# Weighted values of two attention steps in one block, with three buffers of probabilities

## The reference

```
h = layernorm(x) * (1 + ca) + sa                      # x: 4 x 1024 x 256
qkv = h @ w_qkv.T + b_qkv                             # 16 heads of 16
attn = softmax(q @ k.T / sqrt(16))                    # 4 x 16 x 1024 x 1024
x = x + ga * ((attn @ v) @ w_o.T + b_o)
... # a second layer norm, routing of each token to 6 of 32 experts, shared expert
```

## Time and profile before

| | us |
|---|---|
| median of 3 runs | 1539.56 |
| lowest and highest | 1530.76, 1542.15 |
| span of the profiled execution (first to last instruction) | 1412.3 |
| median less span | 127.3 |
| TensorE busy | 1342.8 (95%) |
| VectorE busy | 1134.9 (80%) |
| ScalarE busy | 753.7 (53%) |

### The profile page before, as it was taken

The page is one execution under the profiler, slowest core; times in us unless marked ns, Lnnn a source line. Parts: engine busy times, 40 slices in busy tenths (PEclk is TensorE's granted clock), DMA queues, the critical chain, the costliest instruction groups (busy, mean ns, idle before and its releaser), DMA issues.

```text
span 1412.3 us, 30839 instructions
## 1 busy us (share of the span) xinstructions
PE 1342.8 (95%) x8191; PEld 672.8 (48%) x8192; DVE 1134.9 (80%) x2823; ACT 753.7 (53%) x1155; POOL 606.9 (43%) x782
## 2 busy tenths in 40 slices
PE   7997999999999999999999999999999999999895
PEld 4552222332333323323333232568788888888551
DVE  7886999999999999999999994566566656656588
ACT  3762477676767676777677768113343433334100
POOL 4000113143644534636346357527755555655300
PEclk9997799999999999999999999999999999999999
DMA  6898355533546345444464355947766665666698
GB/s 218 260 270 216 93 171 133 121 85 83 125 126 156 91 121 149 132 96 107 125 170 117 105 155 176 274 136 234 231 199 206 202 183 177 180 179 178 238 344 337
DMA packets 216958, 243.55 MB, mean 172 GB/s; under 512 B 93948, under 2 KB 181500, under 8 KB 216736
## 3 DMA queue, kind: packets, MB, share of 16 engines
q1 hardware_dynamic: 189328, 166.42, 43.6%
q0 software_dynamic: 21776, 68.07, 13.4%
q10 hardware_dynamic: 5760, 7.87, 1.7%
HBM read 133.98 MB, written 108.28 MB: 172 GB/s over the span
## 4 chain that ended last, share of the span: by engine, by line
PE 71%; DVE 13%; DMA 4%; issue 1%; SPq 1%; ACT 1%; POOL 0%; DVEq 0%; POOLq 0%
PE psO L1174 14%; PE ex_psGU L1682 13%; PE psE L1161 13%; PE psM L1151 9%; DVE piece_max L1048 9%; PE ex_psY L1697 7%; PE ex_psX L1671 3%; PE psM L505 2%; PE ex_psA L1691 2%; PE psGU L1495 1%; DMA wide<-results 1%; PE co_psS L1951 1%; PE late_psGU L1931 1%; PE late_psX L1942 1%; PE psM L524 1%
## 5 line engine op out<-in xcount | busy, mean ns | idle before, releaser
L1048 DVE TENSOR_REDUCE piece_max<-psM 128x1 f32<-128x512 f32 x1024 | 641.9, 680 | 27.3 <-PE psM L1151 24.0
L1115 ACT ACTIVATE wide<-psE 128x1024 f32<-128x1024 f32 x512 | 496.8, 1021 | 206.2 <-PE psE L1161 204.1
L1151 PE MATMUL psM<-wide 48*128 48x512 bf16 x1024 | 324.0, 395 | 19.9 <-DVE piece_max L1048 11.7
L1161 PE MATMUL psE<-wide 49*128 49x512 bf16 (+1 forms) x2048 | 328.7, 380 | 3.2 <-DMA wide<-maxima 2.8
L1763 POOL DMA_INDIRECT results<-vals_inv,places x223 | 213.9, 959 | 150.5 <-DVE vals_inv L1749 86.4
L1174 PE MATMUL psO<-wide 128*32 128x512 f32 x2048 | 273.6, 606 | 0.6 <-ACT wide L1115 0.6
L1151 PEld LDWEIGHTS psM<-wide 48*128 48x128 bf16 x1024 | 78.1, 93 | 348.1 <-DVE piece_max L1048 277.3
L1682 PE MATMUL ex_psGU<-wide,ex_xT 128*128 x892 | 231.3, 382 | 0.8 <-ACT ex_xT L1714 0.7
L1161 PEld LDWEIGHTS psE<-wide 49*128 49x128 bf16 (+1 forms) x2048 | 117.6, 95 | 92.3 <-issue 8.7
L1682 PEld LDWEIGHTS ex_psGU<-wide,ex_xT 128*128 128x128 f32 x892 | 152.1, 190 | 14.6 <-issue 2.3
L1714 ACT ACTIVATE ex_xT<-ex_psX 128x256 f32<-128x256 f32 x223 | 85.3, 383 | 121.3 <-PE ex_psX L1671 118.5
(11 more groups left out here) (281 smaller groups left out, 1262.8 us busy)
## 6 DMA issues: line engine op xcount, KB each, us to landing
wide<-qk_parts SPq DMA_DIRECT2D x384, 64.0 KB
wide<-results SPq DMA_DIRECT2D x16, 1536.0 KB, 9.5
rows<-lists SPq DMA_DIRECT2D x112, 160.0 KB
h2Ts<-lists SPq DMA_DIRECT2D x111, 160.0 KB
qk_parts<-parts SPq DMA_DIRECT2D x32, 384.0 KB, 3.1
xin<-in_x_dram SPq DMA_DIRECT2D x16, 512.0 KB, 4.2
v_values<-vst SPq DMA_DIRECT2D x32, 256.0 KB, 3.5
wide<-v_values SPq DMA_DIRECT2D x16, 512.0 KB
```

The costliest lines, as they stand in the source:

```text
L1048: v.tensor_reduce(piece_max[:, qh, (x * PAIRS + h) * KT // QH + qt, kh:kh + 1], bank_of("piece", PIECES * group + n), AX.X, ALU.max, negat ...
L1115: nc.scalar.activation(probs[:, step % 2, 2 * pair:2 * pair + 2], psE[:, pair], ACT.Exp, scale=HD ** -0.5).then_inc(exp_ok, 1)
L1151: nc.tensor.matmul(bank_of(*user), qa[g][rows, h, qt * P:(qt + 1) * P], ka[g][rows, h, kh * 512:(kh + 1) * 512], start=True, stop=True).th ...
L1161: mm = nc.tensor.matmul(psE[:, pair, x], k[g][part, pair, kt * P:(kt + 1) * P], q[g][part, pair, qh * 512:(qh + 1) * 512], start=(q is qa) ...
```

## The change

`probs` becomes a list of three buffers instead of two. The third stands in `h2Ts`. `weighted_values` is no longer called once in each step for the step before, but twice in a row in each even step, for the two steps before; after the loop it is called for the last two. Exp waits for `summed` to reach step - 2 instead of step - 1. Since `h2Ts` is now in use until the end of attention, the contents of the spare rows move to a part of `x2`, GpSimd waits for `spare_in` before its loop over chunks, and SyncE loads `h2Ts` only once `summed` has reached 255.

```diff
-        probs = env.wide[:, GPART * NG:].rearrange("p (n h q) -> p n h q", n=2, h=HG)
+        probs = [*(env.wide[:, GPART * NG + HG * 512 * n:GPART * NG + HG * 512 * (n + 1)].rearrange("p (h q) -> p h q", h=HG)
+                   for n in range(2)), env.h2Ts[:].rearrange("p n k t -> p (n k) t")]
...
-        spare_to = env.h2Ts[:, 0].rearrange("p k t -> p (k t)").bitcast(I32).rearrange("p (e f) -> p e f", e=E)
+        spare_to = env.x2[:, TPC * (LAST - 1):TPC * LAST].rearrange("p i d -> p (i d)").bitcast(I32).rearrange(
+            "p (e f) -> p e f", e=E)
...
-            sp.wait_ge(spare_in, 16 * (E + 1))
+            sp.wait_ge(summed, ALL - 1)
             for n in range(2):
                 sp.wait_ge(env.h2T_out, 16 * (n + 1))
                 sp.dma_start(env.h2Ts[:, n], env.h2T_d[n]).then_inc(env.h2T_in[n], 16)
...
             add_bias(0)
+            pool.wait_ge(spare_in, 16 * (E + 1))
             for c in range(LAST):
...
                     if pair == 0:
-                        wait(act, summed, step - 1)
-                    nc.scalar.activation(probs[:, step % 2, 2 * pair:2 * pair + 2], psE[:, pair], ACT.Exp,
+                        wait(act, summed, step - 2)
+                    nc.scalar.activation(probs[step % 3][:, 2 * pair:2 * pair + 2], psE[:, pair], ACT.Exp,
                                          scale=HD ** -0.5).then_inc(exp_ok, 1)
...
-                                          probs[:, s % 2, 2 * pair + x], start=(kt == 0), stop=(kt == KT - 1))
+                                          probs[step % 3][:, 2 * pair + x], start=(kt == 0), stop=(kt == KT - 1))
...
-                if step:
+                if step and step % 2 == 0:
+                    weighted_values(step - 2)
                     weighted_values(step - 1)
                 if to < NGR:
                     piece(to, first + 2)
                     piece(to, first + 3)
                 route_products(step)
+            weighted_values(ALL - 2)
             weighted_values(ALL - 1)
```

## The result

| | us |
|---|---|
| before, median of 4 runs | 1540.74 (1530.76 to 1542.15) |
| after, median of 4 runs | 1631.07 (1628.08 to 1636.37) |
| ratio, 95% interval | 1.0605 [1.0548, 1.0662] |
| profiled execution after | 1630.02, span 1628.3, mean granted clock 0.956 |

The change costs 90.3 us. The prediction said 1629.6.

The account below looks back on a forecast made before the run. The prediction took a loop through TensorE and VectorE, 2.49 us a step, to bound attention. Terms 79.5 + 7 + 2.5 + 1 = +90 us gave a span of 1502, with 127.3 around it 1629.6 us; range 1612 to 1650.

Parts of the forecast that it names:

- the step from P1 to P2: In plain even steps, TensorE's piece 2 starts 2.22 us behind piece 1, with two sets of weighted values between.
- the loop of a pair: Two plain attention steps, through TensorE and VectorE: 5.80 us against 4.97 before, a price of +0.82 us a pair.
- the lower bound named for this term: Price of a plain pair if the second set's passes come 0.43 us apart: +0.78 us.
- blocks beside other work of VectorE's: Where VectorE selects experts, steps 26 to 29 of a window, its work fills the gap: about 0.1 us a block.
- exp's wait, the spare rows and the loads: Looser exp wait and GpSimd's new wait: zero each; later loads of `h2Ts` behind attention: +1 us, bounds 0 and +4.
- the loops together: Attention's longer pairs: 79.5 us for 97 plain pairs, 7 for other blocks, 2.5 for the last 11 steps.
- the mixed steps: Steps 12 and 30 of a window, gap partly filled: 0.4 and 0.5 us; with the expert-selection blocks +7 us in all.
- the clock: Rival: TensorE's granted clock drops for a tenth of the time in attention, +35 us, 1665 us; chance 0.03.
- 60% of filled places at a clock of 1.00: Evidence against a clock drop: from 405 to 417 us TensorE's places fill some 60% of the step at full clock.
- with 127.3 around the span: Time taken to lie outside the profiled span, 127.3 us, added to the predicted span of 1502 us.
- the first rival: In attention, with VectorE work banked for the block, saved array switches make it faster: -23 us, 1516 us; chance 0.03.

Follow-up runs that it names:

- the occasion at 1417 us: The runs of the first seven experiments, where the unedited kernel before takes 1417 to 1419 us; the result and the last five experiments have it at 1540 to 1545.
- the stand-in: The changed kernel with blocks of two only in steps 26 and 28 of windows 1 to 6, single sets elsewhere: 1541.26 us against 1541.95 for the kernel before.

## Why the prediction was right, and where not

**Right: the step from P1 to P2 and the loop of a pair.** P2 is 2.17 us behind P1 (2.22 predicted), its reduction 0.42 behind it, the rest of the loop as written: 5.74 us for 5.80. The passes of the second set are 0.43 apart and those of the first 0.45, so the lower bound named for this term holds, +0.78. Taking the block away brings the old time back, 24 plain blocks cost 17.0 us where 24 times the price is 18.5, and one bank less costs one reduction a step. The mechanism is shown.

**Right: blocks beside other work of VectorE's.** Twelve of them changed the time by -0.7 us, where +0.1 each was predicted; neither can be told from nothing. **Right: exp's wait, the spare rows and the loads**: 0.5 us with everything in place but the blocks, and 0.6 us more on the chain behind attention with them; +1 was predicted, and neither can be told from nothing.

**Mis-sized: the loops together.** 79.5 + 7 + 2.5 = 89 predicted, some 82 or 83 measured, by the 0.04 to 0.05 us a pair of the second set's passes, 97 times, and a rest of some 2 or 3 us in the mixed steps.

**Wrong: the clock**, given 0.03, +35 us, with "the clock should stay at 1.00". It falls to half in 12 to 14 stretches of attention and costs about 29 us on the occasion at 1417 us, where it was counted; on that of the result, where a kernel with hardly a block has six such stretches itself, the change adds some 10 us by it (an estimate). The step that failed is the evidence taken from the earlier trace rows: 60% of filled places at a clock of 1.00. The block changes how idle time lies, not only how much of it there is: places that were spread now lie closer, with longer pauses between. That this is what brings the fall is my reading and is not shown: 6 of 14 such pauses bring none, and three falls have none ahead. What is shown is that a fall that meets a block doubles 1.86 us and starves VectorE for 2.56. As a rival it had about the right size for the occasion at 1417 us and too small a chance. The same paragraph has the active share of a plain pair fall from 87% to 75%, which was reason for a wider range upward.

**Wrong: "with 127.3 around the span".** Some 2 us lie around a span. The profile and the timed runs were of two occasions, and the 127.3 us were a longer time inside the span of the timed runs: the stand-in's span there is 1535.7 us, with 751.0 in attention and 452.9 in the expert loop for 726.3 and 372.1. On the occasion of the profile the sum should have read 90 - 7 (loops) + 29 (clock) = 112, near the difference of the two spans (1528.1 - 1414.9 = 113.2; the medians differ by 106). On that of the result the clock adds only some 10, and the two errors, -7 and +10, nearly cancel. So +90 met +90.3 by errors of opposite sign. The loop's price is confirmed by itself; that the totals agree to 1.5 us is luck.

**Wrong in its condition: the first rival.** It made the price hang on VectorE alone; for plain steps the prediction has no loop through ScalarE. That did no harm to its number, since this loop, at 5.47 us, is shorter than the one that it had. With VectorE's work halved the pair is held at 5.47 by `psE`, and with ScalarE's halved too the pair is no shorter than before, by the 0.25 us that P3 waits for its bank. The rule of the Trainium skill (TensorEngine Tiling (Array Packing), Key Properties) that a change of the tiling mode drains TensorE agrees in kind with the 0.09 us out of the block, which is paid once a pair now. That the saved switch can be turned into time is not shown by any order tried here.

## What to carry to other kernels

Before merging two pieces of work into a longer block, set what each consumer has banked against the time until its next piece is ready. Here three unread pieces, the first already begun, kept VectorE busy for 1.65 us from P1 on, and the next reduction could start only 0.31 + 1.86 + 0.42 = 2.6 us behind P1. Then look for the next loop (here two buffers of scores and 1.94 us of exps): a saving on an engine counts only when no loop through that engine holds the pace, and side-by-side issue can be lost in the same edit. A sum made against a profile should have its span laid beside the timed runs first; a gap of 9% between them is itself a thing to explain and not a constant to add.

## What was not expected of the hardware

- The granted clock fell to half for 3.4 or 6.8 us at a time in attention, 14 times in one execution of the changed kernel, with no pause of TensorE above 1.04 us there. The kernel before had one such stretch on that occasion, and a kernel with twelve blocks had six on the other.
- Two sets of weighted values one behind the other, with a new semaphore wait between them, go on at the rhythm within a set (0.43 and 0.45 us a pass); only the way in and out of the shape costs its 0.1 and 0.09 us.
- The same program takes 373 or 456 us for the same expert loop on different occasions, with waits of 3 to 5 us that the profile puts down to another core or an unknown queue.
